# Larger score tiles, row sums from the exponentials, and one spreading product in a windowed attention

## What is computed

```python
q, k, v = (qkv[:, :, 0], qkv[:, :, 1], qkv[:, :, 2])
scores = einsum('bshd,bswhd->bshw', q, k_win) / sqrt(16)
scores = where(valid, scores, -1e9)            # |s - w| <= 32
attn = softmax(scores, axis=-1)
out = einsum('bshw,bswhd->bshd', attn, v_win)
x = x + out @ w_out + b_out
```

## Time and profile before

| | us |
|---|---|
| median of 3 runs (3123.58 to 3134.05) | 3124.59 |
| the profiled execution | 3155.56 |
| its span, first to last instruction | 3153.7 |

### The profile page before, as it was taken

How to read it: one execution, slowest core, us unless ns; L and a number is a source line. 1 busy time by engine, 2 the same in 40 slices (tenths; PEclk the granted TensorE clock), 3 DMA queues, 4 the chain that set the end, 5 groups by cost and what they waited for, 6 DMA issues and landing times.

```text
span 3153.7 us, 84405 instructions
## 1 busy us (share of the span) xinstructions
PE 2771.0 (88%) x30287; PEld 2124.4 (67%) x30287; DVE 1942.3 (62%) x4491; ACT 1818.7 (58%) x3661; POOL 1283.4 (41%) x1252
## 2 busy tenths in 40 slices
PE   6989899989989984999999948888888888888897
PEld 4666666666666663999999936666666666666665
DVE  4788888888777885222222215666666666666665
ACT  4767777767676773444444425555555555555554
POOL 1365555565555555000000045445454444555540
PEclk9999999999999996999999969999999999999998
DMA  3122222222222212777777721111111111111110
GB/s 125 68 92 84 81 80 75 75 91 84 80 81 75 75 31 64 228 230 227 230 229 228 228 75 38 47 46 45 44 44 44 44 44 44 44 45 44 44 34 28
DMA packets 139575, 284.62 MB, mean 90 GB/s; under 512 B 25440, under 2 KB 82784, under 8 KB 135392
## 3 DMA queue, kind: packets, MB, share of 16 engines
q1 hardware_dynamic: 114912, 245.68, 24.3%
q0 software_dynamic: 24576, 37.80, 4.5%
HBM read 215.08 MB, written 68.29 MB: 90 GB/s over the span
## 4 chain that ended last, share of the span: by engine, by line
PE 40%; DVE 8%; issue 7%; POOL 3%; DMA 1%; another core or an unknown queue 1%; ACT 1%; DVEq 0%; SPq 0%; POOLq 0%; ACTq 0%
PE psum L1154 9%; PE psum L1145 8%; PE psum L1540 4%; PE psum L1499 4%; PE psum L1570 2%; PE psum L1582 2%; DVE c L1964 2%; PE psum L1557 2%; PE psum L1516 2%; PE psum L1524 2%; POOL ycho L1451 2%; PE psum L1504 1%; PE psum L1550 1%; PE psum L1136 1%; DVE inv L1843 1%
## 5 line engine op out<-in xcount | busy, mean ns | idle before, releaser
L1451 POOL DMA_INDIRECT ycho<-expert_out,place x384 | 359.3, 936 | 668.5 <-DVE place L1829 585.0
L1019 POOL DMA_INDIRECT expert_in<-rows,slot_i x384 | 445.7, 1161 | 132.3 <-issue 111.5
L1188 ACT ACTIVATE hid<-psum,w_blk 128x256 f32<-128x256 f32 x608 | 268.9, 473 | 326.5 <-PE psum L1145 326.5
L1752 ACT ACTIVATE ex<-psum,smin 128x80 f32<-128x80 f32 x1152 | 281.9, 333 | 204.7 <-DVE smin L1836 204.6
L489 PE MATMUL psum<-xn,w_in 128*128 128x288 f32 x1024 | 306.0, 423 | 33.1 <-issue 12.0
L1472 POOL TENSOR_TENSOR qdiag<-qs,parity 128x128 f32<-128x128 f32 x288 | 114.4, 402 | 507.2 <-PE psum L1550 327.9
L1843 DVE RECIPROCAL inv<-psum 128x64 f32<-128x64 f32 x288 | 158.9, 552 | 240.5 <-PE psum L1582 165.2
L1154 PE MATMUL psum<-w_blk,hid 128*128 128x128 f32 x2432 | 296.6, 275 | 0.0
L1540 PE MATMUL psum<-keys,qdiag 32*32 32x80 f32 x9216 | 267.4, 233 | 31.3 <-issue 22.9
L1145 PE MATMUL psum<-x_t,w_blk 128*128 128x256 f32 x1216 | 289.5, 381 | 2.0 <-DMA w_blk<-w_exp_in 2.0
L995 POOL TENSOR_TENSOR unit<-unit 128x576 f32<-128x576 f32 x64 | 121.9, 1905 | 401.6 <-ACT unit L656 292.7
(11 more groups left out here) (240 smaller groups left out, 5928.4 us busy)
## 6 DMA issues: line engine op xcount, KB each, us to landing
w_blk<-w_exp_in SPq DMA_DIRECT2D x152, 578.0 KB, 4.0
xin<-x_in SPq DMA_DIRECT2D x32, 1716.0 KB
rows_in<-expert_in SPq DMA_DIRECT2D x152, 128.0 KB, 2.5
expert_out<-rows_out SPq DMA_DIRECT2D x152, 128.0 KB, 3.4
h_dram<-h SPq DMA_DIRECT2D x32, 288.0 KB
x_dram<-x SPq DMA_DIRECT2D x32, 288.0 KB
h1c<-h_dram SPq DMA_DIRECT2D x32, 288.0 KB
x2c<-x_dram SPq DMA_DIRECT2D x32, 288.0 KB
```

The lines of the kernel that those rows point to most:

```text
L1019: pool.indirect_dma_start(out=expert_in[:, :], out_offset=bass.IndirectOffsetOnAxis(ap=slot_i[z.s][:, n:n + 1], axis=0), in_=rows[z.s][:, ...
L1188: nc.scalar.activation(hid[b.s][:, c, :], HB[b.s][c % HK], ACT.Gelu_apprx_tanh, bias=w_blk[b.q][:, FF + FC * D + c:FF + FC * D + c + 1]).t ...
L1451: pool.indirect_dma_start(out=ycho[x.s][:, k, :], out_offset=None, in_=expert_out[:, :], in_offset=bass.IndirectOffsetOnAxis(ap=place[x.s] ...
L1752: done = nc.scalar.activation(ex[u][:, b, in_window(qb)], score_bank(u)[:, b * QK:(b + 1) * QK], ACT.Exp, bias=smin[u % RING][:, b:b + 1], ...
```

## The change

A tile of the scores gets 64 channels, four heads, instead of 32. The mask by head (`quad`) has four columns, the query tile 4 x 16 columns for each block, and a block has two products of 64x64 weights. The rows of the scores come out as before.

The row sums come from ScalarE: each exponential also gives the sum of its row (`accum_out`, `esum`). VectorE takes their reciprocal, 4 columns (`einv`), and multiplies it into a 0/1 pattern (`block_row`), which gives `inv_rows` with 4 x 16 columns (`inverses`). One product with a block matrix of ones (`head_block`, 128x128) spreads them to the channels of each head; it takes the place of the eight row-sum products and of the reciprocal of 64 columns. `halves` and `heads` do the rest as before; the last product of `heads` reads the spread inverses from PSUM. The value products now wait for the whole of `att` of the unit before (`att_ready`), and for `inv_step`. One subtraction on 4x16 values in `pick_expert` is written in another form.

```diff
+        "head_block": (p[:, None] // HD == p[None, :] // HD),
+        "block_row": (p[:, None] % QB == np.arange(QB)[None, :]),
...
-        qdiag = ring_c("qdiag", [128, UB, 2, QB])
+        qdiag = ring_c("qdiag", [128, UB, QH, QB])          # QH = 4
...
-                    for t in range(NT):
-                        at = slice(t * PH, (t + 1) * PH)
+                    for t in range(HEADS // QH):
+                        at = slice(t * QH * HD, (t + 1) * QH * HD)
                         nc.tensor.matmul(bank[at, b * QK:(b + 1) * QK],
...
-                    pe.wait_ge(head_step, x.upto(HEAD * NU, HEAD * u))
+                    pe.wait_ge(att_ready, x.upto(NU, u))
                 pe.wait_ge(ext_ready, x.upto(NU, u + 1))
-                for j in range(2):
-                    for t in range(NT):
-                        at = slice(t * PH, (t + 1) * PH)
-                        nc.tensor.matmul(sum_bank()[at], pair_ones[:, j, :],
-                                         ex_t[u % RING][:, :, t * PH + j * QB:t * PH + (j + 1) * QB],
-                                         start=(j == 0), stop=(j == 1))
+                pe.wait_ge(inv_step, x.upto(2 * NU, 2 * u + 2))
+                nc.tensor.matmul(sum_bank(), C("head_block"), inv_rows[u % RING][:], start=True, stop=True)
...
-                                                ACT.Exp, bias=smin[u % RING][:, b:b + 1], scale=-1.0)
+                                                ACT.Exp, bias=smin[u % RING][:, b:b + 1], scale=-1.0,
+                                                accum_out=esum[u % RING][:, b:b + 1])
...
+            def inverses(x, u):
+                v.wait_ge(ex_ready, x.upto(NU, u + 1))
+                if u or x.old(1):
+                    v.wait_ge(inv_step, x.upto(2 * NU, 2 * u))
+                v.reciprocal(einv[:], esum[u % RING][:]).then_inc(inv_step, 1)
+                v.wait_ge(inv_step, x.upto(2 * NU, 2 * u + 1))
+                if u >= RING or x.old(1):
+                    v.wait_ge(pv_done, x.upto(NU, u + 1 - RING))
+                v.tensor_tensor(inv_rows[u % RING][:], einv[:].unsqueeze(2).to_broadcast([128, UB, QB]),
+                                C("block_row").unsqueeze(1).to_broadcast([128, UB, QB]), ALU.mult).then_inc(inv_step, 1)
...
-                v.reciprocal(inv[:], sum_bank()).then_inc(head_step, 1)
...
-                                one_head[:], inv[:], ALU.mult).then_inc(att_ready, 1)
+                                one_head[:], sum_bank(), ALU.mult).then_inc(att_ready, 1)
...
                     heads(x, 0)
                     minimum(x, 3)
+                    inverses(x, 1)
...
-            v.tensor_scalar(l16[:], l16[:], m16[:, 0:1], None, ALU.subtract).then_inc(pick_step, 1)
+            v.tensor_tensor(l16[:], l16[:], m16[:].to_broadcast([NI, E2]), ALU.subtract).then_inc(pick_step, 1)
```

More of the change, by code:

```diff
@@ L46 @@
 HD = D // HEADS
+QH = 4
 WIN = 32
@@ L212, in build @@
         band, ident_h = sb("band", [128, cw["band"][1]], BF16), sb("ident_h", [128, 128], BF16)
-        parity, pair_ones = sb("parity", [128, 2]), sb("pair_ones", [KW, 2, 2 * HD])
+        parity = sb("parity", [128, 2])
+        quad = sb("quad", [128, QH])
         place = [sb(f"place{s}", [G, 2 * NG], I32) for s in range(2)]
@@ L1234, in b_vector @@
             v.tensor_reduce(parity[:], C("head_rows").rearrange("p (t j) -> p j t", j=2), AX_X, ALU.add)
-            for j in range(2):
-                v.memset(pair_ones[:, j, j * HD:(j + 1) * HD], 1.0)
-                v.memset(pair_ones[:, j, (1 - j) * HD:(2 - j) * HD], 0.0)
+            v.tensor_reduce(quad[:], C("head_rows").rearrange("p (t j) -> p j t", j=QH), AX_X, ALU.add)
             v.tensor_scalar(q_neg[:], V("q_b"), -float(HD) ** -0.5, None, ALU.mult).then_inc(c_ready, 1)
@@ L1298, in build @@
         val = one_c("val", [KW, IMGS * NWIN, D])
-        qdiag = ring_c("qdiag", [128, UB, 2, QB])
+        qdiag = ring_c("qdiag", [128, UB, QH, QB])
         ex = [one_c(f"ex{u}", [128, UB, KW]) for u in range(NU)]
         smin, ex_t = ring_c("smin", [128, UB]), ring_c("ex_t", [KW, UB, 128])
-        inv, half, one_head = (one_c(name, [128, UB, QB]) for name in ("inv", "half", "one_head"))
+        esum, einv, inv_rows = ring_c("esum", [128, UB]), one_c("einv", [128, UB]), ring_c("inv_rows", [128, UB, QB])
+        half, one_head = (one_c(name, [128, UB, QB]) for name in ("half", "one_head"))
         att = one_c("att", [128, T])
@@ L1322, in build @@
         out_step, out_stored = sem("out_step"), sems("out_stored")
-        zeroed = sem("zeroed")
-        HEAD = 3
+        zeroed, inv_step = sem("zeroed"), sem("inv_step")
+        HEAD = 2
         PICK = 9
@@ L1474, in diagonal @@
                     qs[x.s][:, u * UB * QB:(u + 1) * UB * QB].rearrange("p (b q) -> p b q", b=UB).unsqueeze(2)
-                    .to_broadcast([128, UB, 2, QB]),
-                    parity[:].unsqueeze(1).unsqueeze(3).to_broadcast([128, UB, 2, QB]),
+                    .to_broadcast([128, UB, QH, QB]),
+                    quad[:].unsqueeze(1).unsqueeze(3).to_broadcast([128, UB, QH, QB]),
                     ALU.mult).then_inc(qdiag_ready, 1)
@@ L1880, in step @@
                     minimum(y, 8)
+                    inverses(y, 7)
                     halves(y, 6)
@@ L1884, in step @@
                     heads(y, 7)
+                    inverses(y, 8)
                 if x:
@@ L1902, in step @@
                     minimum(x, 2)
+                    inverses(x, 0)
                 if z:
@@ L1914, in step @@
                     minimum(x, 4)
+                    inverses(x, 2)
                     heads(x, 1)
@@ L1922, in step @@
                     minimum(x, 5)
+                    inverses(x, 3)
                 if w:
@@ L1935, in step @@
                     minimum(x, 6)
+                    inverses(x, 4)
                 if y:
@@ L1944, in step @@
                     minimum(x, 7)
+                    inverses(x, 5)
                 if w:
@@ L1950, in step @@
                                     two(r4[:]).rearrange("p g (m n) -> p g m n", m=2), ALU.mult).then_inc(xq_ready, 1)
+                if x:
+                    inverses(x, 6)
             c_steps(v, step)
```

6 lines of the change are left out of this document (4 added, 2 removed).

## The result

The changed kernel takes 3204.01 us (median of 4 runs, 3201.07 to 3205.36) where the kernel before takes 3126.41 beside it: a ratio of 1.0243, 95% interval 1.0223 to 1.0263. It is slower by 78 us; the forecast was 35 us faster, and its range ended at 3185.

What follows compares the result with a forecast made beforehand. TensorE's stalls in bursts of tiny products and a step closing over GpSimd were taken as the bounds. Per step -3.6 + 1.1 + 1.0 + 0.3 = -1.2 us, over 30 steps -35, gave 3090 us; range 3045 to 3185.

Steps and rivals of the forecast that it cites:

- The stalls go, 3.6 us a step.: TensorE's score blocks and a late signal, third stage: fewer tiny instructions end the idle time, 3.6 us a step (bounds 0, 3.6).
- The stalls stay: Rival: TensorE's stalls have another cause, so only costs of 2.4 us a step remain; 3160 to 3197 us, chance 0.24.
- VectorE: nearly nothing in sum.: VectorE loses a 552 ns reciprocal and gains one of 141 and a product of 258: nearly nothing in sum.
- The port: nothing in sum.: VectorE instructions with two SBUF inputs beside GpSimd: att loses one, the inverses' product has two; nothing in sum.
- A new wait, 1.0 us each, one counted.: TensorE's spreading product waits for VectorE's inverses at two places a step, 1.0 us each; one lies beside GpSimd's chain.
- Reads: 0.36 us a unit, 1.1 a step.: ScalarE's accumulator reads after exponentials: 0.36 us a unit, at three places on the path, 1.1 us a step.
- GpSimd's query tile, 0.3.: GpSimd's query tile grows from 128 to 256 columns; once a step in the closing chain, 0.3 us more.
- The floor of 25 ns: About 25 ns between TensorE instruction starts, however small; would save 0.4 us a unit, but a 16 ns row opposes it.
- The 31 us between the profiled execution and the median: Profiled execution 3155.56 against median 3124.59: at most 1 us a step of what was read is the profile's own.
- the idle time by issue of the score weights: Sign in the new profile: TensorE's score weight loads idle by issue fall from 106.3 to under 20 us.

Runs made afterwards that it cites:

- e3: The kernel before with the 64x64 score tiles alone; 3137.66 us, ratio 0.9952.
- e4: The changed kernel with the 32x32 score tiles of before, so the row sums' part alone; 3207.18 us, ratio 1.0261.
- f1: The changed kernel with 80 one-column memsets on VectorE once ahead of the third stage, which move its loop body; 3050.25 us, ratio 1.0195.
- e8: The changed kernel with four of VectorE's inverses moved earlier and VectorE's third stage written out step by step; 3139.68 us, ratio 0.9953.
- e5: The changed kernel with four of VectorE's inverses moved earlier; 3168.24 us, ratio 1.0146, and in another job 3194.03 us, ratio 1.0125.
- f2: The changed kernel with four inverses moved earlier and 80 memsets on VectorE once ahead of the third stage; 3044.78 us, ratio 1.0177.
- b_before_again: The kernel before, unchanged, run once more in the fifth job; 2988.62 us, ratio 0.9993.
- a_after_third: The changed kernel, unchanged, run once more in the fourth job; 3087.88 us, ratio 1.0319.
- f3: The kernel before with 25 small VectorE memsets in every step and 22 more once ahead of the third stage; 3032.13 us, ratio 1.0130.
- p25_small: The kernel before with 25 one-column memsets on VectorE in every step of the third stage; 3156.91 us, ratio 1.0006.

## Why the prediction was wrong

**"The stalls go, 3.6 us a step."** By size this is the step that failed most. The blocks became whole, as the forecast said, and the gain did not follow. e3 gives 15 us, 0.5 us a step, and the tiles on top of the row sums 5 us (after against e4), so some 3 us of the 3.6 never came. The cause that I inferred, too many tiny instructions, is not borne out: with half as many score products signals are as late (1.9 us at 2502.29), and on another chip the same 32 products never stall. It is something of the chip or its surroundings, and what, stays open. The forecast had this as a rival ("The stalls stay", chance 0.24, 3160 to 3197); what was measured lies beyond it, since the costs beside it were more than the 2.4 us a step that it counted.

**"VectorE: nearly nothing in sum."** This is the term that was missing. I counted VectorE's time and not its code. Per step 26 instructions came, waits and register work included (two-step body 240 to 292), and the body came to lie where the jump back fetches it again. Price: 38 us beside f1, 54 beside e8 where the inverses are early. A rival of this kind was missing. It could have been had from what lay open: the built program, the length of the body, and the page of the skill named above.

**A rough account.** Some 3 us a step of gain fall away, 90 us with 30 steps, and the jump back costs 38 to 54: 128 to 144 us over the forecast, where 113 were measured. The terms are from different chips, and some of them hide behind each other. So these two suffice for the miss, but the exact shares on the result's chip aren't shown.

**"The port: nothing in sum."** The rule was right and I applied it at the wrong place. I looked at what stands between GpSimd's sum and xq, and not at unit 4's inverses, which stand beside the weighting and have TensorE waiting. It takes 2.52 us instead of 0.23, some 2 us a step on the result's chip. The Trainium skill ("SBUF — State Buffer", "Who interferes with whom") says that a VectorE instruction with two SBUF inputs contends with a GpSimd instruction that reads SBUF, and the trace agrees: the tile ends with the weighting.

**"A new wait, 1.0 us each, one counted."** The size was exact (0.93 idle, twice a step). Together with unit 4's wait they are worth the 34 us of e5 on the one chip, 1.1 us a step; without unit 4's, 5 us of f2 on the other, where GpSimd's chain and the clock take the rest.

**"Reads: 0.36 us a unit, 1.1 a step."** Four exponentials with their reads take 1.35 us, against 0.98, as forecast. The runs' price of 0.8 us a step rests on two ratios of different chips, so it is no more than in line.

**"GpSimd's query tile, 0.3."** 618 ns where 0.72 was forecast. Its share on the path isn't separated: with the tiles alone the one step at full clock takes 34.6 us against 34.1.

**TensorE's clock had no term.** In the trace of after an inner step has 4.0 us at the lower granted clock, in that of before 1.6. Such a stretch of 3.4 us makes a step 1.0 to 1.5 us longer (before: 39.0 against 40.0; b_before_again: 34.1 against 35.6). So 0.7 to 1.0 us a step of the loss, an estimate, came by way of the clock. It is no further item of the account above, since the times measured there contain it.

**The floor of 25 ns**, which the forecast had named, does not show here either: 16 value products start within 0.36 us (trace of after, 2539.56 to 2539.92), 22 ns each.

**The 31 us between the profiled execution and the median**, which the forecast put down to the profile at most, were more likely those of another chip: the medians of the kernel before are 3152 and 3155 in the first and third job.

What the forecast's last part wanted to see did come (blocks of 0.7, reads at 1.35, waits of 1 us twice), but the idle time by issue of the score weights fell only to 74.3, not under 20, and that was the sign that it was not what I took it for: on the fast chip it is 55.5 in the unchanged kernel, with no stall in a block.

None of these kernels beats the kernel before on every chip. e8 and e3 are 0.5% under before where it takes 3152 to 3155; on the chips of 2989 both the tiles alone and the early inverses with moved code are 1.8 to 2.0% over it. e8 was not run there.

## What to carry to other kernels

When a change adds instructions to an engine's loop, count its body in the built program: with 240 it was safe here, with 288 to 292 it hung on where the body lay, and instruction packets inside the loop are the sign. A product that an engine waits for should neither have two SBUF inputs beside a long GpSimd operation nor stand behind a minimum that needs the latest product; moving it up brought 34 us on one chip and 5 on another. A gain that rests on gaps "by issue" needs a look at a second chip before it enters a sum. And compare steps at the same granted clock before you say what a change is worth: the tiles alone on the fifth job's chip lost by it, and the early inverses of f2 lost most of their gain.

## What the runs showed of the hardware

- A jump back to code that had to be fetched held VectorE for 2.97 to 3.25 us in after and a_after_third (0.75 to 1.07 in f3, and longer behind it), and brought 5 packets of 8 KB; elsewhere the same jump takes 0.38 or nothing. The same instructions moved by 80 places are 38 us faster. Those of another kernel moved by 22 places have the packets where they had none before (f3 and p25_small, 1.0130 and 1.0006 on two chips).
- The unchanged kernel takes 2989 us on two chips and 3126 to 3155 on three, with equal durations of its single instructions (the score products' weights: mean 105 ns in both). The difference is in idle time, and 142 of 170 us of it in the third stage (before and b_before_again: 1208 and 1066 us).
- TensorE's granted clock was 0.50 after a wait of 2.56 us in one kernel and 1.00 after one of 2.44 in another. A stretch of 3.4 us at the lower level made a step of 34.1 us 1.5 longer.
